# Decoder layer in three stages on one core: GpSimd's second root moves ahead of the addition of the recurrence's input

## The chip, the cores and the metric

The kernel runs on one core of a Trainium2 chip. A core has five engines that work from their own instruction queues: PE (TensorE), DVE (VectorE), ACT (ScalarE), POOL (GpSimd) and SP (SyncE, which only issues DMAs). The metric is the device time of one execution in microseconds (us), the median of several runs.

## The reference

32 sequences of 256 tokens with 256 channels go through three post-norm sublayers:

```
x = layernorm(x + conv.real * x)          # a complex linear recurrence, one state per channel
x = layernorm(x + xattn(x, ctx))          # 16 heads of 16 channels, 256 queries x 256 keys, with its own layer norm
x = layernorm(x + ffn(x))                 # RMS norm, nearest of 8 centroids picks one expert, gated MLP of width 512
```

The recurrence runs over the first axis of `x`, the 32 sequences: `state = c * state + x[n]`, and each needs the one before it. In the third sublayer every token is computed by one expert only, so the kernel sorts tokens by expert.

## The kernel before

Phase 1 (0 to about 850 us of the span) handles one item, a sequence, per step of a software pipeline, for the recurrence, the attention and the choice of the expert. Phase 2 runs the experts on 71 tiles of 128 sorted tokens. There is no scheduler: each engine's program is written out by hand as a function `step(t)`, each operation is for an item t+3, t+2, ... or t-3, and the engines meet through semaphores only (`wait(engine, name, item, per)` before an operation, `then_inc` behind it). So an engine works strictly in the order that its own `step` has, and a wait holds everything that is written behind it.

A step has 16 heads. On PE, head h is `scores` (L1078, into bank S of PSUM, two banks for alternate heads) and `transposed_scores` (L1091, bank T, for the item before). DVE takes the maximum over each S bank (`maxima`, L1312), ACT the exponential of each T bank. Heads are issued in pairs, (0,1), (2,3), and so on, and all the other work of the step stands between the pairs. A bank S is written again only when its maximum has been taken.

The work around the change, in the order of one step:

- DVE, end of step t: the slot of each token of item b = t-3 (L1498, `slot`), the residual y2 of item a = t-2 (L1393), its statistics (L1296) and, behind the maxima of heads 12 to 15, their moments (L1302, written to `mv2`, semaphore `ln2`).
- DVE, start of step t+1: maxima of heads 0 and 1; then `row`, the normalised y2 (L1327, two instructions), which waits for `rstd2`; a copy of the token numbers (L1329); maxima of heads 2 and 3; then `u = (state + 1) * x` (L1335), which waits for all five parts of the recurrence (`conv`).
- POOL, whole step t: `conv_products` (L705, `by_re`, twice as large as the others), `weigh` (L763, `xw`), the bias (L806), `cut` (L794) for the queries, `offset` (L785), `conv_real` (L713), the root for the first layer norm (L738, L740), `conv_imag` (L721, L724) around a `cut` for the keys, the root for the attention's own layer norm (`rstdx`), `scatter` (L775, two indirect DMAs, waits for `slot_ok`), `conv_input` (L731, adds x to `state`), the root for the second layer norm (`rstd2`, L738 and L740) and `rms` (L749 to L755, four tiny operations). The next step begins with L705 again.
- `offset` (L785) writes the constant part of the distances to the centroids. DVE's `pick` (L1461) waits for it behind the maxima of heads 6 and 7. Later in the step DVE adds the queries (L1443) and forms `onehot_bf` (L1478).

`rstd` adds epsilon (L738) and raises to the power of -0.5 (L740):

```
wait(pool, ready, item, per)
g.tensor_scalar(rs[:, 0], mv[:, :, 1], LN_EPS, None, ALU.add).then_inc(s[done], 1)
```

Of the kernel before, what the change touches and what calls it, by code (L numbers as in the profile page):

```python
# [81 lines left out]
def build(nc, x, ctx_in, lmlg, theta, last_conv, Wq, bq, Wk, bk, Wv, bv, ln_g, ln_b, ffn_scale, centroids, up_w, down_w, out):  # L82
    stack = ExitStack()
    with stack:
# [36 lines left out]
        def sb1(name, shape, dt=F32):  # L121
            return phase1.enter_context(nc.sbuf_tensor(name, shape, dt))
# [67 lines left out]
        mv2 = sb1("mv2", [P, NTC, 2])  # L190
        rs2 = sb1("rs2", [P, 2, NTC])
# [38 lines left out]
        def wait(eng, name, item, per=1, j=None):  # L230

            if not item.runtime and item.k >= SEQ:
                item, j = Item(0, SEQ - 1), per
            wait_value(eng, name, item.times(per, per if j is None else j))
# [11 lines left out]
        def wait_ring(eng, sm, item, ring, per):  # L246

            if not item.runtime:
                while item.k >= SEQ:
                    item = item - ring  # L250
            wait_value(eng, sm, item.uses(ring) * per)
# [11 lines left out]
        def active(item):  # L263
            return item.within(0, SEQ)
# [275 lines left out]
        with nc.Block() as block:  # L540
# [121 lines left out]
            def _(pool):  # L662
# [35 lines left out]
                def conv_products(item):  # L698

                    if not active(item):  # L700
                        return
                    wait(pool, "conv", item - 1, 5)
                    if item.k == 1:
                        wait(pool, "x1_ok", item - 1, 2)
                    g.tensor_tensor(by_re[:, :, :, :], state[:, 0].unsqueeze(1).to_broadcast(both), pair_b, ALU.mult).then_inc(s["conv"], 1)  # L705

                def conv_real(item):

                    if not active(item):
                        return  # L710
                    wait(pool, "conv", item, 5, 1)
                    wait(pool, "u_ok", item - 1)
                    g.tensor_tensor(state[:, 0], by_re[:, 1], state[:, 1], ALU.subtract).then_inc(s["conv"], 1)  # L713

                def conv_imag(item, j):

                    if not active(item):
                        return
                    if j == 0:
                        wait(pool, "conv", item, 5, 2)  # L720
                        g.tensor_tensor(state[:, 1], state[:, 1], re_b, ALU.mult).then_inc(s["conv"], 1)  # L721
                    else:
                        wait(pool, "conv", item, 5, 3)
                        g.tensor_tensor(state[:, 1], state[:, 1], by_re[:, 0], ALU.add).then_inc(s["conv"], 1)  # L724

                def conv_input(item):
                    if not active(item):
                        return
                    wait_ring(pool, x_in[item.mod(2)], item, 2, 16)
                    wait(pool, "conv", item, 5, 4)  # L730
                    g.tensor_tensor(state[:, 0], state[:, 0], xt[:, item.mod(2)], ALU.add).then_inc(s["conv"], 1)  # L731

                def rstd(item, ready, per, mv, rs, done):

                    if not active(item):
                        return
                    wait(pool, ready, item, per)
                    g.tensor_scalar(rs[:, 0], mv[:, :, 1], LN_EPS, None, ALU.add).then_inc(s[done], 1)  # L738
                    wait(pool, done, item, 2, 1)
                    g.tensor_tensor(rs[:, 1], rs[:, 0], neg_half[:, :].to_broadcast([P, NTC]), ALU.pow).then_inc(s[done], 1)  # L740

                def rms(item):

                    if not active(item):
                        return
                    p = item.mod(2)
                    wait(pool, "rstd2", item, 2)
                    wait_ring(pool, scat[p], item - 2, 2, 16 * NTC)
                    g.tensor_tensor(ms2[:, 0], mv2[:, :, 1], rs2[:, 1], ALU.mult).then_inc(s["rms"], 1)  # L749
                    wait(pool, "rms", item, 4, 1)  # L750
                    g.tensor_tensor(ms2[:, 1], ms2[:, 0], rs2[:, 1], ALU.mult).then_inc(s["rms"], 1)
                    wait(pool, "rms", item, 4, 2)
                    g.tensor_scalar(ms2[:, 2], ms2[:, 1], RMS_EPS, None, ALU.add).then_inc(s["rms"], 1)
                    wait(pool, "rms", item, 4, 3)
                    g.tensor_tensor(row[:, p, :, C], ms2[:, 2], neg_half[:, :].to_broadcast([P, NTC]), ALU.pow).then_inc(s["rms"], 1)  # L755

                def weigh(item):

                    if not active(item):
                        return  # L760
                    wait(pool, "x2_ok", item, 2)
                    wait(pool, "nx_ok", item - 1, 2)
                    g.tensor_tensor(xw[:, :, :], row[:, item.mod(2), :, 0:C], scale_bc[:, :].unsqueeze(1).to_broadcast([P, NTC, C]),  # L763
                                    ALU.mult).then_inc(s["xw_ok"], 1)

                def scatter(item):

                    if not active(item):
                        return
                    p = item.mod(2)  # L770
                    wait(pool, "slot_ok", item, SLOT)
                    wait(pool, "id_ok", item)
                    wait(pool, "rms", item, 4)
                    for c in range(NTC):
                        g.indirect_dma_start(out=buckets[:, :], out_offset=bass.IndirectOffsetOnAxis(ap=slot[:, p, c:c + 1], axis=0),  # L775
                                             in_=row[:, p, c, :], in_offset=None, bounds_check=PAD - 1,
                                             oob_is_err=False).then_inc(scat[p], 16)

                def offset(item):

                    if not active(item):
                        return
                    wait(pool, "nx_ok", item, 2)
                    wait(pool, "pick", item - 1, PICK, 2)
                    g.tensor_tensor(dist[:, 0], cent_norm[:, :].unsqueeze(1).to_broadcast([P, NTC, E]),  # L785
                                    nx[:, :].unsqueeze(2).to_broadcast([P, NTC, E]), ALU.add).then_inc(s["offset"], 1)

                def cut(item, src, hi, lo, ready, done, out):

                    if not active(item):  # L790
                        return
                    wait(pool, ready, item, 4)
                    wait_ring(pool, out[(item - 1).mod(2)], item - 1, 2, 32)
                    g.tensor_tensor(lo[:, :, :], src, hi[:, :, :].bitcast(F32), ALU.subtract).then_inc(s[done], 1)  # L794

                def step(t):
                    n, a, b = t + 1, t - 2, t - 3
                    first = t.k < 0
                    if first:
                        rstd(t + 2, "ln1", 4, mv1, rs1, "rstd1")  # L800
                    conv_products(t + 3)
                    weigh(b)
                    if active(a):
                        wait(pool, "x1_ok", a, 2)
                        wait(pool, "x1T_pe", a)
                        g.tensor_tensor(x1[:, a.mod(4)], x1[:, a.mod(4)], b_bc[:, :].unsqueeze(1).to_broadcast([P, NTC, C]),  # L806
                                        ALU.add).then_inc(s["x1b_ok"], 1)
                    if n.k > 0:
                        cut(n, q32[:, :, :], q_hi, q_lo, "q_ok", "q_cut", q_out)
                    offset(b)  # L810
                    conv_real(t + 3)
                    if not first:
                        rstd(t + 2, "ln1", 4, mv1, rs1, "rstd1")
                    conv_imag(t + 3, 0)
                    if n.k + 1 > 0:
                        cut(n + 1, k32[:, :, :], k_hi, k_lo, "k_ok", "k_cut", k_out)
                    conv_imag(t + 3, 1)
                    rstd(a, "lnx", 4, mvx, rsx, "rstdx")
                    if t.k < SEQ:
                        scatter(b)  # L820
                    conv_input(t + 3)
                    rstd(a, "ln2", 4, mv2, rs2, "rstd2")
                    rms(a)
                    if t.k >= SEQ:
                        scatter(b)

                steps(pool, step)
                gpsimd2(pool)

# [703 lines left out]
```

## Time and profile before

| | |
|---|---|
| median of 3 runs | 1241.71 us (1241.17 to 1245.56) |
| the profiled execution, own time | 1245.21 us |
| its span in the profile | 1243.4 us |
| mean granted TensorE clock | 0.943 of full speed |
| PE busy | 1110.6 us (89%) |
| DVE busy | 955.3 us (77%) |
| POOL busy | 775.6 us (62%) |
| ACT busy | 668.9 us (54%) |

Busy time is an average over both phases. Phase 1 and phase 2 have different limits, and the change touches phase 1 alone. Times inside the trace are counted from the start of the span.

### The profile page before, as it was taken

The numbers are of one execution on the slowest core, as the hardware profiler recorded it, in microseconds if no ns is written. First come the engines' busy times: TensorE is split into PE (matmuls) and PEld (weight loads), VectorE is DVE, ScalarE is ACT, GpSimd is POOL, SyncE is SP. The second block draws the span as 40 slices with busy tenths as digits, with TensorE's granted clock in tenths as the row PEclk, the third lists the DMA queues.
The fourth block names the chain that finished last, engine by engine and source line by source line (L and its number), as shares of the span: only waits on it lengthen the run. The fifth ranks groups of instructions, "written<-read, shape, count | busy, mean of one in ns | idle before, by whom it ended". The sixth has DMA issues, their size and how long they took to land.

```text
span 1243.4 us, 27486 instructions
## 1 busy us (share of the span) xinstructions
PE 1110.6 (89%) x8030; PEld 818.2 (66%) x8061; DVE 955.3 (77%) x2416; ACT 668.9 (54%) x1416; POOL 775.6 (62%) x932
## 2 busy tenths in 40 slices
PE   3899989999999999989999998853999999999996
PEld 2566666666666666656666666532888888888885
DVE  7458988999989999999999998845555555555553
ACT  4257666767767767767767767541222222222221
POOL 4646879889979888978978955450333333333333
PEclk9679999999999999999999998656999999999998
DMA  4667667766556556556556554042111111111110
GB/s 128 162 162 205 178 179 208 188 148 161 148 134 163 142 142 163 147 138 163 144 141 163 134 130 109 11 153 60 48 51 48 43 51 51 50 47 49 50 52 19
DMA packets 90825, 144.91 MB, mean 117 GB/s; under 512 B 12662, under 2 KB 78335, under 8 KB 84512
## 3 DMA queue, kind: packets, MB, share of 16 engines
q1 hardware_dynamic: 83616, 126.09, 39.2%
q0 software_dynamic: 6528, 16.99, 4.7%
q8 instruction: 55, 0.90, 0.3%
q10 hardware_dynamic: 576, 0.53, 0.2%
q14 instruction: 50, 0.41, 0.1%
HBM read 91.44 MB, written 53.03 MB: 116 GB/s over the span
## 4 chain that ended last, share of the span: by engine, by line
PE 42%; DVE 33%; issue 9%; DMA 6%; POOL 6%; SPq 2%; ACT 1%; POOLq 0%; DVEq 0%; ACTq 0%
DVE neg_max_sb L1312 12%; PE Y L454 10%; PE G L422 8%; PE A L422 8%; DVE oq L1443 4%; DVE u L1335 3%; PE S L1078 3%; DMA neg_max<-nm_row 3%; PE GT L432 2%; PE O L1027 2%; POOL buckets L775 2%; PE M L1035 2%; POOL state L731 2%; DVE st L1296 2%; DVE stx L1296 2%
## 5 line engine op out<-in xcount | busy, mean ns | idle before, releaser
L1312 DVE TENSOR_REDUCE neg_max_sb<-S 128x2 f32<-128x512 f32 x512 | 327.5, 681 | 46.9 <-PE S L1078 46.1
L909 ACT ACTIVATE probs<-T 128x512 f32<-128x512 f32 x512 | 278.1, 595 | 141.0 <-PE T L1091 127.7
L1078 PE MATMUL S<-k_st,q_st 48*128 48x256 f32 x1024 | 215.0, 319 | 38.0 <-DVE neg_max_sb L1312 34.9
L1078 PEld LDWEIGHTS S<-k_st,q_st 48*128 48x128 f32 x1024 | 146.3, 192 | 115.4 <-issue 77.1
L1091 PE MATMUL T<-q_st,k_st 49*128 49x256 f32 x1024 | 211.3, 319 | 6.3 <-DMA q_st<-neg_max 2.6
L1091 PEld LDWEIGHTS T<-q_st,k_st 49*128 49x128 f32 x1024 | 146.4, 192 | 22.8 <-ACT probs L909 15.4
L399 ACT ACTIVATE gT<-GT 128x512 f32<-128x512 f32 x71 | 42.5, 598 | 207.8 <-PE GT L432 207.8
L1027 PE MATMUL O<-probs,v_aug 128*32 128x256 f32 x2048 | 145.6, 404 | 0.8 <-ACT probs L909 0.7
L378 POOL DMA_INDIRECT out<-res,token x71 | 76.5, 1077 | 103.3 <-DVE res L503 98.8
L454 PE MATMUL Y<-dn_sb,gT 128*128 x568 | 134.2, 379 | 0.8 <-ACT gT L399 0.8
L454 PEld LDWEIGHTS Y<-dn_sb,gT 128*128 128x128 f32 x568 | 107.5, 189 | 18.2 <-issue 1.0
L775 POOL DMA_INDIRECT buckets<-row,slot x64 | 67.3, 1052 | 81.9 <-DVE slot L1498 71.8
L422 PE MATMUL G<-up_hi,xsT 128*128 x284 | 107.9, 421 | 1.3 <-DVE xsT L508 1.0
L422 PE MATMUL A<-up_hi,xsT 128*128 x284 | 106.6, 416 | 0.0
L383 POOL TENSOR_SCALAR rs<-mv 128x1 f32<-128x1 f32 x71 | 16.0, 226 | 141.5 <-DVE mv L532 141.4
L503 DVE TENSOR_SCALAR res<-y,mv,rs 128x256 f32<-128x256 f32 x71 | 29.4, 413 | 86.1 <-POOL rs L385 86.1
L1027 PEld LDWEIGHTS O<-probs,v_aug 128*32 128x32 f32 x2048 | 55.4, 113 | 52.8 <-ACT probs L909 16.4
L1035 PE MATMUL M<-ctT,wk_sb 128*128 128x256 f32 x256 | 68.9, 416 | 15.6 <-issue 8.5
L403 ACT ACTIVATE gate<-G 128x512 f32<-128x512 f32 x71 | 42.4, 597 | 59.9 <-PE G L422 59.9
L1054 PE MATMUL M<-wv_sb,ctT 128*128 128x256 f32 x256 | 72.0, 407 | 2.6 <-issue 0.7
L705 POOL TENSOR_TENSOR by_re<-state,decay 128x1024 f32<-128x1024 f32 x31 | 73.5, 2372 | 1.1 <-DVE x L1399 0.9
L1035 PEld LDWEIGHTS M<-ctT,wk_sb 128*128 128x128 f32 x256 | 49.6, 204 | 27.6 <-issue 12.7
(185 smaller groups left out, 2553.9 us busy)
## 6 DMA issues: line engine op xcount, KB each, us to landing
k_st<-k_pieces SPq DMA_DIRECT2D x64, 256.0 KB, 5.1
q_st<-q_pieces SPq DMA_DIRECT2D x64, 256.0 KB, 3.9
xr<-buckets SPq DMA_DIRECT2D x71, 129.0 KB, 2.1
xt<-in_x SPq DMA_DIRECT2D x32, 256.0 KB, 6.1
ct<-in_ctx SPq DMA_DIRECT2D x32, 256.0 KB, 6.8
k_pieces<-k_hi SPq DMA_DIRECT2D x32, 256.0 KB, 3.6
k_pieces<-k_lo SPq DMA_DIRECT2D x32, 256.0 KB, 3.7
q_pieces<-q_hi SPq DMA_DIRECT2D x32, 256.0 KB, 2.1
```

The costliest lines, as they stand in the source:

```text
L378: g.indirect_dma_start(out=out_rows, out_offset=bass.IndirectOffsetOnAxis(ap=token[:, f.mod(2):f.mod(2) + 1], axis=0), in_=res[:, f.mod(2) ...
L422: last = t_.matmul(ps[:, :], xT[:, w, c * P:(c + 1) * P], src[:, bass.ds(off + c * 2 * HID, HID)], start=(k == 0), stop=(k == len(terms) - 1))
L454: last = t_.matmul(Y_ps[:, 0:C], gT[:, m.mod(2), c * P:(c + 1) * P], dn_sb[:, bass.ds(off + c * C, C)], start=(c == 0), stop=(c == HCH - 1))
L705: g.tensor_tensor(by_re[:, :, :, :], state[:, 0].unsqueeze(1).to_broadcast(both), pair_b, ALU.mult).then_inc(s["conv"], 1)
L775: g.indirect_dma_start(out=buckets[:, :], out_offset=bass.IndirectOffsetOnAxis(ap=slot[:, p, c:c + 1], axis=0), in_=row[:, p, c, :], in_of ...
L909: a_.activation(probs[:, h % 8].rearrange("p k t -> p (k t)"), T_ps[h % 2][:, :], ACT.Exp, scale=DH ** -0.5).then_inc(s["exp_ok"], 1)
L1027: last = t_.matmul(O_ps[32 * j:32 * j + 32, (grp % 2) * TOK:(grp % 2 + 1) * TOK], v_aug[:, item.mod(4), kc, h * VW:h * VW + 32], probs[:, ...
L1035: last = t_.matmul(dst[:, oc * TOK:(oc + 1) * TOK], w[:, ic, oc * P:(oc + 1) * P], xT[:, ic, :], start=(ic == 0), stop=(ic == NCH - 1))
L1054: last = t_.matmul(M_ps[1][:, c * C:(c + 1) * C], ctT[:, ic, c * P:(c + 1) * P], wv_sb[:, ic, :], start=False, stop=(c == NTC - 1 and ic = ...
L1078: last = t_.matmul(S_ps[h % 2][:, c * TOK:(c + 1) * TOK], q_st[base:base + STACK, h, c * P:(c + 1) * P], k_st[base:base + STACK, h, :], st ...
L1091: last = t_.matmul(T_ps[h % 2][:, c * TOK:(c + 1) * TOK], k_st[base:base + AUG, h, c * P:(c + 1) * P], q_st[base:base + AUG, h, :], start= ...
L1312: v.tensor_reduce(neg_max[:, cur.mod(2), :, h], S_ps[h % 2][:, :].rearrange("p (c t) -> p c t", c=NTC), AX.X, ALU.max, negate=True).then_i ...
```

## The change

The diff exchanges two calls in GpSimd's step. The root for the second layer norm comes right behind the scatter, and the addition of x to the state comes behind that root. No operation is added, removed or resized, and no wait is.

```diff
                     rstd(a, "lnx", 4, mvx, rsx, "rstdx")
                     if t.k < SEQ:
                         scatter(b)
+                    rstd(a, "ln2", 4, mv2, rs2, "rstd2")
                     conv_input(t + 3)
-                    rstd(a, "ln2", 4, mv2, rs2, "rstd2")
                     rms(a)
```

On POOL, the end of a step in the middle of phase 1 and the start of the next, in the kernel before (`L738`, `L740` with `rs<-mv` are the root, `L731` is the addition of x to the state, `L775` the scatter, `L705` the products of the next item):

```order
L740 TENSOR_TENSOR rsx<-rsx,neg_half 128x2
L775 DMA buckets<-row,slot 66688x258 x2
L731 TENSOR_TENSOR state<-state,xt 128x512
L738 TENSOR_SCALAR rs<-mv 128x2
L740 TENSOR_TENSOR rs<-rs,neg_half 128x2
L749 TENSOR_TENSOR ms<-mv,rs 128x2
L751 TENSOR_TENSOR ms<-ms,rs 128x2
L753 TENSOR_SCALAR ms<-ms 128x2
L755 TENSOR_TENSOR row<-ms,neg_half 128x2
L705 TENSOR_TENSOR by_re<-state,decay 128x1024
```

The same place on POOL in the changed kernel:

```order
L740 TENSOR_TENSOR rsx<-rsx,neg_half 128x2
L775 DMA buckets<-row,slot 66688x258 x2
L738 TENSOR_SCALAR rs<-mv 128x2
L740 TENSOR_TENSOR rs<-rs,neg_half 128x2
L731 TENSOR_TENSOR state<-state,xt 128x512
L749 TENSOR_TENSOR ms<-mv,rs 128x2
L751 TENSOR_TENSOR ms<-ms,rs 128x2
L753 TENSOR_SCALAR ms<-ms 128x2
L755 TENSOR_TENSOR row<-ms,neg_half 128x2
L705 TENSOR_TENSOR by_re<-state,decay 128x1024
```

The two tiny operations of the root have moved ahead of the 128x512 addition. With them the wait for `ln2`, which DVE's moments give, has moved ahead of it too. The programs of PE, DVE and ACT are the same, row for row. DVE's order around it, in both kernels:

```order
L1302 BN_AGGR mv<-st 128x2 x2
L1312 TENSOR_REDUCE neg_max_sb<-S 128x2 x2
L1327 TENSOR_SCALAR row<-oq,mv,rs 128x256 x2
L1329 COPY row<-ids 128x2
L1312 TENSOR_REDUCE neg_max_sb<-S 128x2 x2
L1335 SCALAR_TENSOR_TENSOR u<-state,xt 128x512
```

Nothing has moved here. L1327 is the user of the root and L1335 the user of the addition.

## Rows read from the trace of the kernel before

**Rows 1.** The page: the chain that ended last, shares of the span.

```profile
PE 42%; DVE 33%; issue 9%; DMA 6%; POOL 6%; SPq 2%; ACT 1%; POOLq 0%; DVEq 0%; ACTq 0%
```

**Rows 2.** Busy time of each engine in the stretch 130 to 730 us.

```profile
130.00:730.00 600.00, 553.00 (x4923) 380.72 (x4947) 566.13 (x1432) 426.97 (x941) 513.01 (x564) 0.99 0.61 157
```

The columns are: stretch, its length, busy time of PE, PEld, DVE, ACT and POOL with the number of instructions, granted clock, DMA share, GB/s.

**Rows 3.** Line L1335 (DVE's u): duration ns minimum/median/maximum; busy time, 130 to 730 us.

```profile
L1335 DVE SCALAR_TENSOR_TENSOR u<-state,xt x32: 681/2519/2583, 14.0 to 728.8; 128x512 f32<-128x512 f32 x32
130.00:730.00 600.00, 60.16 (x26) 0.99 0.61 157
```

**Rows 4.** Line L1327 (DVE's row): for whom it waited, us and times.

```profile
  POOL rs L740: 20.6, 29
```

**Rows 5.** Timeline of POOL, 558 to 568.5 us: start, duration, engine, line, operation.

```profile
559.19 1.09 POOL L775 DMA_INDIRECT buckets<-row,slot  x1 [3.26 <-DVE slot L1498]
...
561.58 1.29 POOL L731 TENSOR_TENSOR state<-state,xt 128x512 f32<-128x512 f32 x1
...
563.14 0.72 POOL L740 TENSOR_TENSOR rs<-rs,neg_half 128x2 f32<-128x2 f32 x1
563.94 0.20 POOL L749 TENSOR_TENSOR ms<-mv,rs 128x2 f32<-128x2 f32 x1
...
565.50 2.37 POOL L705 TENSOR_TENSOR by_re<-state,decay 128x1024 f32<-128x1024 f32 x1
```

In brackets stands the idle time ahead of an instruction, and what ended it.

**Rows 6.** Timeline of DVE, 557.9 to 568.5 us.

```profile
558.22 0.16 DVE L1498 CAST slot<-slot_f 128x2 uint32<-128x2 f32 x1
...
561.76 0.24 DVE L1302 BATCH_NORM_AGGREGATE mv<-st 128x2 f32<-128x6 f32 x2
561.92 1.27 DVE L1312 TENSOR_REDUCE neg_max_sb<-S 128x2 f32<-128x512 f32 x2
563.90 0.73 DVE L1327 TENSOR_SCALAR row<-oq,mv,rs 128x256 f32<-128x256 f32 x2 [0.70 <-POOL rs L740]
...
564.68 1.29 DVE L1312 TENSOR_REDUCE neg_max_sb<-S 128x2 f32<-128x512 f32 x2
565.89 2.53 DVE L1335 SCALAR_TENSOR_TENSOR u<-state,xt 128x512 f32<-128x512 f32 x1
```

**Rows 7.** Timeline of PE, 561 to 565 us.

```profile
561.40 0.35 PE L1078 MATMUL S<-k_st,q_st 48*128 48x256 f32 x1 [1.09 <-DVE neg_max_sb L1312]
...
564.37 0.28 PE L1078 MATMUL S<-k_st,q_st 48*128 48x256 f32 x1
```

**Rows 8.** Timeline, 113.2 to 119 us: the first step in which item a exists.

```profile
114.45 0.24 DVE L1302 BATCH_NORM_AGGREGATE mv<-st 128x2 f32<-128x6 f32 x2
...
114.78 0.22 POOL L738 TENSOR_SCALAR rs<-mv 128x2 f32<-128x2 f32 x1 [5.60 <-DVE mv L1302]
...
115.83 0.74 DVE L1327 TENSOR_SCALAR row<-oq,mv,rs 128x256 f32<-128x256 f32 x2
...
117.37 1.29 DVE L1312 TENSOR_REDUCE neg_max_sb<-S 128x2 f32<-128x512 f32 x2 [0.67 <-PE S L1078]
...
117.43 2.37 POOL L705 TENSOR_TENSOR by_re<-state,decay 128x1024 f32<-128x1024 f32 x1
```

**Rows 9.** Timeline, 30.8 to 36 us: a root of 128x2, and what starts behind it.

```profile
31.44 0.72 POOL L740 TENSOR_TENSOR rs<-rs,neg_half 128x2 f32<-128x2 f32 x1
...
32.13 2.35 POOL L705 TENSOR_TENSOR by_re<-state,decay 128x1024 f32<-128x1024 f32 x1
32.19 3.77 DVE L1399 TENSOR_SCALAR x<-u,mv,rs 128x256 f32<-128x256 f32 x2 [1.16 <-POOL rs L740]
```

**Rows 10.** Timeline, 571.5 to 573 us: POOL's offset and DVE's pick.

```profile
571.91 0.21 POOL L785 TENSOR_TENSOR dist<-cent_norm,nx 128x16 f32<-128x16 f32 x1
...
572.24 0.36 DVE L1461 SCALAR_TENSOR_TENSOR dist<-M,row,dist 128x8 f32<-128x8 f32 x2
```

**Rows 11.** Line L1478 (DVE's onehot_bf): duration ns minimum/median/maximum, and its busy time, 130 to 730 us.

```profile
L1478 DVE TENSOR_TENSOR onehot_bf<-expert_no,choice x32: 161/186/1276, 128.3 to 842.5; 128x16 bf16<-128x16 f32 x32
130.00:730.00 600.00, 14.24 (x25) 0.99 0.61 157
```

## The prediction

> **What bounds the kernel now.** I read the page first. The chain that ended last is 42% PE and 33% DVE [rows 1], but that is over two phases, and the change is in the first only. So I took the stretch 130 to 730 us, 26 steps of the steady state (counted by u, 26 times [rows 3]), 600 / 26 = 23.1 us each. There DVE is busy 566.13 us of 600 (94%), PE 553.00 (92%), POOL 513.01 (86%) [rows 2]. Three engines are nearly full, so what matters is which wait of a step ends last, and I read one step, 558 to 568 us, engine by engine.
>
> On POOL the reader is to see a queue without a gap from the scatter on: 559.19 scatter (the only long wait, 3.26 us, for DVE's slot), 561.58 addition to the state, 563.14 root, 563.94 rms, 565.50 by_re, done at 565.50 + 2.37 = 567.87 [rows 5]. On DVE: slot at 558.22, moments done at 561.76 + 0.24 = 562.00, maxima of heads 0 and 1, then row at 563.90 after 0.70 us of waiting for the root, maxima of heads 2 and 3 at 564.68, u at 565.89, which takes 2.53 us [rows 6].
>
> Two things follow. First, u is not working for 2.53 us. It starts 0.39 us behind by_re and ends 0.55 us behind by_re's end (568.42 against 567.87). The same line takes 0.68 us at the least and 2.52 in the median [rows 3]. So the 0.55 us behind by_re are its own streaming, and what is ahead of them is standing. A clearer case of the same thing is early: L1399, whose two instructions take 0.73 us elsewhere, as row's do [rows 6], took 3.77 us when they started 0.06 us behind by_re [rows 9]. A DVE operation of this kind that starts behind a large POOL operation stands until that one ends. In the stretch, u's mean is 60.16 / 26 = 2.31 us [rows 3]; 22 of the 26 that make this sum are over 2.2 us.
>
> Second, row's wait looks like 20.6 us for the taking (29 times, 0.71 us each [rows 4]), but it isn't where the time is lost. The loop that sets a step is: DVE's slot, POOL's scatter to by_re, the end of u, DVE to the next slot. In it POOL has no gap and row doesn't stand.
>
> **The change, part by part.**
>
> *The root comes earlier for DVE.* It can't start when the scatter is done (561.58, where the addition started), since its input is done at 562.00. In the first such step POOL was waiting there, and L738 started at 114.78 for moments done at 114.45 + 0.24 = 114.69, so 0.09 us later [rows 8]. The root starts at 562.09 and takes to 562.09 + 0.32 + 0.72 = 563.13 (L738 to L740 is 0.32: the addition ends at 562.87, its follower starts 0.05 before that end as others of this queue do, at 562.82, and L740 starts at 563.14). That is 0.73 us earlier than 563.86, about all of row's wait. Its worth is nothing: what is behind row is the maximum of head 2, and its scores end on PE at 564.37 + 0.28 = 564.65, against its start at 564.68 [rows 7, 6]. PE worked without a gap from head 1's scores to them. The step at 114 us shows it: there row had no wait, and the maxima waited 0.67 us for PE in its place; from one pair of maxima to the next were 114.61 to 117.37 = 2.76 us, the same as 561.92 to 564.68 [rows 8, 6]. (114.61 is the moments' start 114.45 plus 0.16, as in rows 6.)
>
> *The addition comes later, and with it by_re.* Before, addition, root and rms take 565.50 - 561.58 = 3.92 us to by_re [rows 5]. Afterwards the same work starts at 562.09 instead of 561.58: 0.51 us of POOL waiting, with nothing to cover it. A little comes back, since rms no longer waits for a result just made: from L740 to its dependent L749 are 0.80 us [rows 5], from L740 to an independent by_re only 32.13 - 31.44 = 0.69 [rows 9]. So by_re moves by 0.51 - 0.11 = 0.40 us, to 565.90.
>
> *Row meets the addition.* After the change, row (earliest 563.15) starts about 0.06 us behind the addition (562.09 + 0.32 + 0.69 = 563.10). This is the pattern of rows 9: same form of instruction, same 0.06. L1399's pair there took 3.77 us, and ended each at 0.14 us behind a POOL operation. So row's first half ends at 563.10 + 1.27 + 0.14 = 564.51, against 563.90 + 0.41 = 564.31 before. Maxima of heads 2 and 3 move by 0.20, to 564.88, and u to 566.09. That costs nothing by itself, because u stands behind by_re (565.90) anyway, but its lead decides what follows: by_re is first by 0.19 us.
>
> The Trainium skill, "SBUF — State Buffer", section "SBUF: two separate sides", says that the port pair which DVE and GpSimd share is a lock, held for a whole instruction by whoever starts first, and that a DVE operation with two SBUF inputs needs it against a GpSimd operation that reads SBUF. The trace agrees (3.77 us for 0.73). By that rule alone the order of by_re and u, not their length, sets the price, and the sum below would be the same as long as by_re is first.
>
> *rms meets row's second half.* Bounds: nothing (before, the two overlap too and row takes 0.73 [rows 6]) to about one tiny operation, 0.20 [rows 5]. I take 0.02, near the lower end.
>
> **The sum.** u ends by_re's start + 2.92 (565.50 to 568.42), so each step gets 0.40 + 0.02 = 0.42 us longer, and everything of DVE and POOL behind it moves together. It applies to 22 steps of the stretch and the last u at 728.8 us, 23 in all: 9.7 us. In four steps of the stretch u was short (0.9 to 1.4 us) since PE was late; three of them I count as nothing (bound 0.4 each). The first step has no scatter to wait for: the addition stood in idle time there and moves behind the root, 1.24 us; by_re starts at 117.43 + 1.24, u ends 2.92 behind that start as before: once 1.2 us. Together 10.9 us. The profiled execution would go from 1245.2 to 1256.1; it lay 3.5 us over the median, and against the median it is 1241.7 + 10.9 = 1252.6.
>
> **The rivals.**
>
> *The wait for the root was real: faster (0.08).* If everything on DVE from row on came earlier by row's wait, 26 steps would be 0.70 us shorter each, 18 us: 1223.5. For it speaks that DVE is the busiest engine [rows 2]. The point from which it decides is the end of u: it must come before 568.42. Against it speak PE's end at 564.65, the 0.67 us of waiting at 117.37, and that u ends with by_re, which gets later.
>
> *u overtakes by_re (0.14).* My lead is 0.19 us. If row isn't held up, u is at 565.89 and by_re at 565.90: a tie. Then u takes 0.68 to 566.57 and by_re runs behind it, to about 566.5 + 2.37 = 568.87. The next POOL operation, xw, had to stand behind u's end, 568.42, and now starts at 568.87: 0.45 later, and offset with it. DVE's pick, only 572.24 - 572.12 = 0.12 behind offset's end [rows 10], comes about as much later: 0.45 x 26 + 1 = 12.7 us, 1254.4. DVE's gain of 1.85 us in u turns into waits for PE's scores and for offset. The same page of the Trainium skill, "Who interferes with whom", has it that issue order, not the shape, decides who stands still; the case above is that rule's other outcome.
>
> *The collisions further on change (0.26).* onehot_bf, whose least is 0.16 us, takes up to 1.28 behind a POOL operation. (14.24 - 25 x 0.17) / 1.11 = 9 of 25 steps are long [rows 11], and which of the two engines' waiting operations goes first, with starts some 0.1 us apart, decides it. Phases after by_re stay the same in my forecast, so I expect the same share. If all steps go short (0.10), 9 x 1.11 = 10 us come back: 1242.6, no change. If two thirds go long (0.16), 8 more: 1261.5.
>
> *The chain has slack after all (0.06).* Then the change does nothing: 1241.7. POOL's queue without a gap speaks against it.
>
> *The forecast: 0.46.*
>
> **How the numbers follow.** Half a percent, 6.2 us, is about what a measurement of this kernel tells from no change. Slower by more: 0.46 + 0.14 + 0.16 = 0.76, less 0.05 for a sum that comes out too small (all three bounds at their lower ends give 0.38 x 22 = 8.4, still over 6.2): 0.71. No change: 0.10 + 0.06 + 0.05 = 0.21. Faster: 0.08. The range reaches from the case of all short steps less a little, 1240, to two thirds long plus the upper bound of a step's price (0.60 x 23 = 13.8 for 9.7), 1265. What is left out is the fast rival and a little at both ends.
>
> **What the changed profile would show.** Right if: row's wait for L740 is gone, and row takes about 1.4 us with the addition beside it; the maxima of heads 2 and 3 wait for PE or for row, and start within 2.76 to 3.0 us of those of heads 0 and 1; POOL idles 0.5 us ahead of L738 for DVE's moments; by_re starts 7.68 us behind the start of slot, where it was 565.50 - 558.22 = 7.28; u still takes over 2.2 us. Wrong if u takes 0.7 us (second rival), if onehot_bf's busy time in the stretch moves far from 14 us (third), or if steps get shorter without either (first).

## The result and the profile after

The changed kernel takes **1256.43 us** in the median of four runs (1253.59 to 1262.63), the kernel before 1241.44 in four (1236.99 to 1245.56). The ratio is **1.0128 [1.0075, 1.0182]**: slower by 15.0 us, and the interval leaves out both no change and half a percent. The profiled execution took 1254.54 us, its span is 1252.7, and the mean granted TensorE clock is 0.947, against 0.943 before. A ratio with its interval, here and below, is not the quotient of the two medians given beside it (1.0121 here). Executions that are over 1.5% longer than the fastest one of the same kernel are left out of a ratio, though not out of the medians: four of ten in the third experiment, two of five in the eighth, and one of the 21 of the kernel before in the last four.

The chain that ended last, on the page of the changed kernel:

```profile
DVE 44%; PE 42%; issue 8%; DMA 2%; SPq 1%; ACT 1%; POOL 1%; DVEq 0%; POOLq 0%; ACTq 0%
```

PE has the same 42% as in [rows 1], and DVE has 44% in place of 33%. That is a trap: the engine that the change slowed is POOL, and POOL's share fell to 1%. The chain is followed back along whoever ended a wait. Before, row waited for the root, and there the chain went over to POOL and back to the scatter. Now row waits for nobody, so the chain stays on DVE, where row and u stand behind POOL operations as *busy* instructions, and a busy instruction is put down to its own engine. The stretches below say it more plainly.

Busy time in 130 to 730 us, first of every engine, then of DVE in u (L1335), row (L1327) and onehot_bf (L1478) alone:

```profile
130.00:730.00 600.00, 545.95 (x4867) 375.52 (x4866) 586.77 (x1404) 422.49 (x926) 500.90 (x551) 0.99 0.61 154
...
130.00:730.00 600.00, 71.32 (x25) 0.99 0.61 154
...
130.00:730.00 600.00, 42.39 (x50) 0.99 0.61 154
...
130.00:730.00 600.00, 14.16 (x25) 0.99 0.61 154
```

Against [rows 2], PE and POOL do less in the same 600 us (the steps are longer: u stands in it 25 times for 26), and DVE is busy 586.77 for 566.13 though it too has fewer. The added busy time is standing: u takes 71.32 / 25 = 2.85 us for 60.16 / 26 = 2.31 [rows 3], and row's pair 42.39 / 25 = 1.70 us for 0.73 [rows 6]. onehot_bf is as before: 14.16 for 14.24 [rows 11].

For whom row waited, in the whole run:

```profile
  POOL rs L740: 3.6, 4
```

Before it was 20.6 us in 29 waits [rows 4]. So 17.0 us of DVE's waiting are gone, and the kernel is 15 us slower.

One step on POOL; [rows 5] have the same step of before:

```profile
564.29 1.09 POOL L775 DMA_INDIRECT buckets<-row,slot  x1 [1.60 <-DVE slot L1498]
565.68 0.97 POOL L775 DMA_INDIRECT buckets<-row,slot  x1 [0.30 <-issue]
567.19 0.22 POOL L738 TENSOR_SCALAR rs<-mv 128x2 f32<-128x2 f32 x1 [0.54 <-DVE mv L1302]
567.50 0.72 POOL L740 TENSOR_TENSOR rs<-rs,neg_half 128x2 f32<-128x2 f32 x1
568.20 1.28 POOL L731 TENSOR_TENSOR state<-state,xt 128x512 f32<-128x512 f32 x1
569.44 0.24 POOL L749 TENSOR_TENSOR ms<-mv,rs 128x2 f32<-128x2 f32 x1
...
571.07 2.38 POOL L705 TENSOR_TENSOR by_re<-state,decay 128x1024 f32<-128x1024 f32 x1
```

And on DVE:

```profile
563.32 0.15 DVE L1498 CAST slot<-slot_f 128x2 uint32<-128x2 f32 x1
...
566.87 0.24 DVE L1302 BATCH_NORM_AGGREGATE mv<-st 128x2 f32<-128x6 f32 x2
567.02 1.27 DVE L1312 TENSOR_REDUCE neg_max_sb<-S 128x2 f32<-128x512 f32 x2
568.25 1.70 DVE L1327 TENSOR_SCALAR row<-oq,mv,rs 128x256 f32<-128x256 f32 x2
...
569.94 1.27 DVE L1312 TENSOR_REDUCE neg_max_sb<-S 128x2 f32<-128x512 f32 x2
571.14 2.85 DVE L1335 SCALAR_TENSOR_TENSOR u<-state,xt 128x512 f32<-128x512 f32 x1
...
577.81 0.36 DVE L1461 SCALAR_TENSOR_TENSOR dist<-M,row,dist 128x8 f32<-128x8 f32 x2
```

The reader is to see four things. POOL idles 0.54 us ahead of L738, where it had no gap. by_re starts 571.07 - 563.32 = 7.75 us behind slot, for 7.28 in [rows 5, 6]. Row starts 0.05 us behind the addition (568.25 against 568.20) and takes 1.70 us without a wait. u starts 0.07 behind by_re and ends at 573.99, 0.54 behind by_re's end (573.45); it was 0.55 before. pick (L1461) follows at 14.49 behind slot, for 14.02 in [rows 6, 10]. The 0.47 us at by_re, which is where the change ends on POOL, is found again 7 us later without loss. From the first u of the steady part to the last, 26 steps later, are 115.1 to 737.5 = 622.4 us, before 118.6 to 728.8 = 610.2: 12.2 us more, 0.47 a step. The two profiled spans differ by only 9.3 us, since the profiled execution of the changed kernel came to that first u 3.5 us earlier.

The steps aren't all of one length, and the shortest ones tell the change best: from one by_re to the next they are 22.69 us before and 23.15 after. Over the 24 steps from 141.45 to 704.32 us before, and from 138.51 to 714.24 after, the changed kernel takes 12.86 us more, of which 24 x 0.46 = 11.0 us is this floor. The other 1.8 us lie in the steps that are longer than it, by a long onehot_bf or by a late PE.

### The profile page after: what moved, and what is told of

Its sections match the earlier page's. It is cut to its first block, busy times and chain, and to the rows that moved or that the text cites. A ratio compares the mean times of both kernels' runs of the same rounds, so it can differ in the third digit from the quotient of the medians.

```text
span 1252.7 us, 27516 instructions
## 1 busy us (share of the span) xinstructions
PE 1110.0 (89%) x8060; PEld 816.2 (65%) x8061; DVE 990.2 (79%) x2416; ACT 671.8 (54%) x1416; POOL 770.9 (62%) x932
## 4 chain that ended last, share of the span: by engine, by line
DVE 44%; PE 42%; issue 8%; DMA 2%; SPq 1%; ACT 1%; POOL 1%; DVEq 0%; POOLq 0%; ACTq 0%
DVE neg_max_sb L1312 17%; PE Y L454 10%; PE G L422 8%; PE A L422 8%; DVE oq L1443 4%; PE M L1035 3%; DVE u L1335 3%; DVE st L1296 3%; DVE row L1327 3%; PE S L1078 3%; PE GT L432 2%; DVE oq L1393 2%; PE O L1027 2%; DVE x L1399 2%; DVE stx L1296 2%
## 5 line engine op out<-in xcount | busy, mean ns | idle before, releaser
L1312 DVE TENSOR_REDUCE neg_max_sb<-S 128x2 f32<-128x512 f32 x512 | 326.5, 679 | 38.7 <-PE S L1078 38.5
L1078 PE MATMUL S<-k_st,q_st 48*128 48x256 f32 x1024 | 212.2, 315 | 41.3 <-DVE neg_max_sb L1312 38.1
L1078 PEld LDWEIGHTS S<-k_st,q_st 48*128 48x128 f32 x1024 | 143.7, 189 | 118.2 <-issue 78.3
L775 POOL DMA_INDIRECT buckets<-row,slot x64 | 67.3, 1051 | 84.9 <-DVE slot L1498 74.9
L1035 PE MATMUL M<-ctT,wk_sb 128*128 128x256 f32 x256 | 76.1, 449 | 29.2 <-issue 22.7
L1035 PEld LDWEIGHTS M<-ctT,wk_sb 128*128 128x128 f32 x256 | 54.4, 223 | 43.3 <-issue 27.7
L1335 DVE SCALAR_TENSOR_TENSOR u<-state,xt 128x512 f32<-128x512 f32 x32 | 79.3, 2477 | 0.0
L705 POOL TENSOR_TENSOR by_re<-state,decay 128x1024 f32<-128x1024 f32 x31 | 73.6, 2376 | 1.2 <-DVE x L1399 0.9
```

What stands on the lines that cost most here:

```text
L1035: last = t_.matmul(dst[:, oc * TOK:(oc + 1) * TOK], w[:, ic, oc * P:(oc + 1) * P], xT[:, ic, :], start=(ic == 0), stop=(ic == NCH - 1))
L1078: last = t_.matmul(S_ps[h % 2][:, c * TOK:(c + 1) * TOK], q_st[base:base + STACK, h, c * P:(c + 1) * P], k_st[base:base + STACK, h, :], st ...
L1312: v.tensor_reduce(neg_max[:, cur.mod(2), :, h], S_ps[h % 2][:, :].rearrange("p (c t) -> p c t", c=NTC), AX.X, ALU.max, negate=True).then_i ...
L1335: v.scalar_tensor_tensor(u[:, :, :], state[:, 0], 1.0, xt[:, nn.mod(2)], ALU.add, ALU.mult).then_inc(s["u_ok"], 1)
```

## The experiments

In the experiments "before" is the kernel before, run again on the same chip. All numbers relative to slot are from steps near 560 us. In the changed kernel every step of the stretch repeats them within 0.03 us: by_re starts 7.74 to 7.76 us behind slot, pick 14.47 to 14.52.

### The wait alone, without the move

The order of before; only the wait for DVE's moments is put ahead of the addition. Line numbers behind it are 2 higher.

```diff
                         scatter(b)
+                    if active(a):
+                        wait(pool, "ln2", a, 4)
                     conv_input(t + 3)
                     rstd(a, "ln2", 4, mv2, rs2, "rstd2")
```

What was expected:

> The order of the kernel before, with one thing of the change alone: GpSimd waits for the moments (ln2) ahead of the addition to the state; the root stays behind the addition, so vector's row isn't served earlier and doesn't meet the addition. Theory one (the wait in GpSimd's gapless queue from the scatter to by_re is the cost): by_re comes about 0.5 us later behind slot (7.28 becomes 7.8), u still takes over 2.5 us, row waits some 1.2 us for the root in place of 0.70, a short step is 22.68 + 0.5 = 23.2 us, and the run is about 12 us slower than before, as the changed kernel. Rival (row's collision with the addition, 1.70 us for 0.73, is the cost): here row takes 0.73, and the time is that of the kernel before within 3 us.

Measured: 1261.26 us (1258.22 to 1265.13, 4 runs), before 1245.92 (13 runs), ratio **1.0132 [1.0101, 1.0163]**. POOL's timeline of this kernel:

```profile
570.35 1.27 POOL L731 TENSOR_TENSOR state<-state,xt 128x512 f32<-128x512 f32 x1 [0.53 <-DVE mv L1304]
571.60 0.22 POOL L738 TENSOR_SCALAR rs<-mv 128x2 f32<-128x2 f32 x1
...
574.26 2.38 POOL L705 TENSOR_TENSOR by_re<-state,decay 128x1024 f32<-128x1024 f32 x1
```

DVE's timeline of the same step:

```profile
566.48 0.16 DVE L1500 CAST slot<-slot_f 128x2 uint32<-128x2 f32 x1
...
572.65 0.74 DVE L1329 TENSOR_SCALAR row<-oq,mv,rs 128x256 f32<-128x256 f32 x2 [1.19 <-POOL rs L740]
...
574.57 2.62 DVE L1337 SCALAR_TENSOR_TENSOR u<-state,xt 128x512 f32<-128x512 f32 x1
```

by_re starts 7.78 us behind slot. Nothing was reordered, row isn't held by the addition (0.74), and the slowdown is that of the changed kernel. So the 0.53 us for which POOL waits for the moments is a sufficient cause. Row's collision with the addition isn't needed for it.

### The root and rms both ahead of the addition

```diff
                         scatter(b)
-                    conv_input(t + 3)
                     rstd(a, "ln2", 4, mv2, rs2, "rstd2")
                     rms(a)
+                    conv_input(t + 3)
```

What was expected:

> Root, then rms, then the addition to the state, all behind the scatter. The same total of GpSimd's work behind the same wait, but only tiny operations beside row. Theory one: by_re as in the changed kernel (7.7 behind slot); row takes 0.73 and the maxima of heads 2 and 3 wait for PE; u needs the addition, which ends about when by_re can start, so the two meet; time 8 to 15 us over the kernel before. Rival (row's collision is the cost): about the kernel before. Second rival (row's gain of 0.7 us is worth something as long as nothing eats it): up to 18 us faster than before, since row's wait is gone here with no collision in its place.

Measured: 1260.46 us (1257.58 to 1263.91, 4 runs), ratio **1.0108 [1.0080, 1.0135]**. DVE's timeline:

```profile
568.50 0.16 DVE L1498 CAST slot<-slot_f 128x2 uint32<-128x2 f32 x1
...
573.45 0.74 DVE L1327 TENSOR_SCALAR row<-oq,mv,rs 128x256 f32<-128x256 f32 x2
...
574.98 1.29 DVE L1312 TENSOR_REDUCE neg_max_sb<-S 128x2 f32<-128x512 f32 x2 [0.66 <-PE S L1078]
576.42 2.91 DVE L1335 SCALAR_TENSOR_TENSOR u<-state,xt 128x512 f32<-128x512 f32 x1 [0.15 <-issue]
```

Here row has neither a wait nor a collision. It is done 0.66 us before the maxima of heads 2 and 3 can start, and they wait for PE's scores in its place. So an early row is worth nothing, as the prediction had it, and the kernel is as slow as with the collision. What both share is POOL's wait; by_re starts 7.90 behind slot.

### The addition ahead of the scatter

```diff
+                    conv_input(t + 3)
                     if t.k < SEQ:
                         scatter(b)
-                    conv_input(t + 3)
                     rstd(a, "ln2", 4, mv2, rs2, "rstd2")
```

What was expected:

> The addition to the state stands ahead of the scatter, in the 1.6 to 3.3 us in which GpSimd waits for slot; behind the scatter only root and rms. Theory one: by_re comes about 6.5 us behind slot in place of 7.28, so u ends some 0.7 us earlier, less about 0.5 us that the addition takes from vector's two-input operations beside it (L1450, L1393): 0 to 10 us faster than before, most likely 5. Row's wait is gone and the maxima of heads 2 and 3 wait 0.6 us for PE. Rival (row's wait was the price, whatever by_re does): 18 us faster than before. If GpSimd's queue isn't what sets the step: slower than before by the new collisions, some 10 us.

Measured: 1254.47 us in the median of ten runs (1238.54 to 1268.99), which scatter more than those of any other kernel here; ratio **1.0015 [0.9977, 1.0054]**. The median of all ten lies 0.7% above the kernel before, and the longest had a granted clock of 0.919 where the shortest had 0.938. Whether the kernel brings that about itself isn't shown, so a small loss isn't excluded. POOL's timeline:

```profile
535.70 1.27 POOL L731 TENSOR_TENSOR state<-state,xt 128x512 f32<-128x512 f32 x1
537.81 1.09 POOL L775 DMA_INDIRECT buckets<-row,slot  x1 [0.84 <-DVE slot L1498]
...
540.72 0.22 POOL L738 TENSOR_SCALAR rs<-mv 128x2 f32<-128x2 f32 x1 [0.55 <-DVE mv L1302]
...
543.38 2.37 POOL L705 TENSOR_TENSOR by_re<-state,decay 128x1024 f32<-128x1024 f32 x1
```

DVE's slot in the same step:

```profile
536.35 0.65 DVE L1498 CAST slot<-slot_f 128x2 uint32<-128x2 f32 x1
```

POOL still waits 0.55 us for the moments, but the addition's 1.24 us are out of the chain and lie where POOL waited for slot. In return slot itself stands 0.49 us behind the addition (0.65 us for 0.16). The sum is 7.75 - 1.24 + 0.49 = 7.00 from slot to by_re; 543.38 - 536.35 = 7.03 was measured. The expectation had 6.5: it had the addition hold up other operations of DVE, not slot itself. It was 7.28 in the kernel before, but only about 0.1 us of the 0.25 comes through to the shortest steps (22.5 to 22.6 us for 22.7), and no gain is measured: PE is next. The maxima wait for it 36.8 us in the stretch (35 times). Before it was:

```profile
  PE S L1078: 8.4, 9
```

### u ahead of row, in the kernel before

DVE's u moves from behind the maxima of heads 2 and 3 to ahead of row, so that it runs before by_re starts.

```diff
                             maxima(cur, h + 1)
+                        if h == 0 and active(nn):
...
+                            v.scalar_tensor_tensor(u[:, :, :], state[:, 0], 1.0, xt[:, nn.mod(2)], ALU.add, ALU.mult).then_inc(s["u_ok"], 1)
                         if h == 0 and active(b):
                             wait(dve, "rstd2", b, 2)
...
-                        if h == 3 and active(nn):
...
-                            v.scalar_tensor_tensor(u[:, :, :], state[:, 0], 1.0, xt[:, nn.mod(2)], ALU.add, ALU.mult).then_inc(s["u_ok"], 1)
```

What was expected:

> GpSimd as before; vector computes u ahead of row, in the 0.70 us in which it waited for the root, and so ahead of by_re. If by_re and u standing in one another's way is what makes u 2.5 us long: u takes 0.7 to 1.4 us here and row is at most 0.7 us later, the maxima of heads 4 and 5 start up to 0.65 us earlier (then PE's scores stop them), xw isn't behind u any more and offset comes 0.4 us earlier; pick waits for offset. A step gets 0.4 to 0.5 us shorter, the run about 11 us faster than before, 1230 us. If u's length is its own and not by_re's: u takes 2.5 us here too and the run is slower than before by up to 2 us a step.

Measured: 1256.44 us (1254.46 to 1259.28, 4 runs), ratio **1.0091 [1.0067, 1.0114]**. The expectation of a gain was wrong. DVE's timeline:

```profile
569.48 0.68 DVE L1328 SCALAR_TENSOR_TENSOR u<-state,xt 128x512 f32<-128x512 f32 x1
570.78 0.74 DVE L1333 TENSOR_SCALAR row<-oq,mv,rs 128x256 f32<-128x256 f32 x2 [0.62 <-POOL rs L740]
...
574.08 1.29 DVE L1312 TENSOR_REDUCE neg_max_sb<-S 128x2 f32<-128x512 f32 x2 [1.28 <-PE S L1078]
...
578.66 0.36 DVE L1461 SCALAR_TENSOR_TENSOR dist<-M,row,dist 128x8 f32<-128x8 f32 x2 [0.52 <-POOL dist L785]
```

POOL's timeline of the same step:

```profile
569.50 1.24 POOL L740 TENSOR_TENSOR rs<-rs,neg_half 128x2 f32<-128x2 f32 x1
...
572.38 2.37 POOL L705 TENSOR_TENSOR by_re<-state,decay 128x1024 f32<-128x1024 f32 x1
```

Line L1478 (onehot_bf) in 130 to 730 us, with the minimum, median and maximum duration in ns:

```profile
L1478 DVE TENSOR_TENSOR onehot_bf<-expert_no,choice x25: 163/1248/1267, 149.3 to 727.4; 128x16 bf16<-128x16 f32 x25
```

u takes 0.68 us for 2.5, so DVE is 1.8 us earlier there. All of it goes: u starts 0.02 us ahead of the root, and the root takes 1.24 us for 0.72, so by_re comes 7.80 behind slot (slot is at 564.58), 0.5 later than before. The maxima of heads 4 and 5 then wait 1.28 us for PE, pick waits 0.52 us for POOL's offset, and onehot_bf is long nearly always: 29.12 us in the stretch where it was 14.24, and its median is 1248 ns for 186 [rows 11]. Not all of these cost the same. At pick only 0.06 us of the half microsecond at by_re is left (578.66 - 564.58 = 14.08 behind slot for 14.02), since xw no longer stands behind u, while onehot_bf is long in 23 of 25 steps for 9, 14 more at 1.1 us. That is the bulk of the slowdown. So both mechanisms that the second and the third rival name exist, one engine or the other going first and a different share of long onehot_bf; the change under study starts neither.

### The changed kernel with earlier moments, and its control

If POOL's wait is the cause, the change must cost nothing once the moments are there in time. On DVE the statistics of y2 are taken ahead of x1 (L1399) and the moments ahead of the maxima of heads 14 and 15, in the changed kernel and, as a control, in the kernel before.

```diff
+                        if h == 13 and active(a):
+                            wait(dve, "y_ok", a, 4)
+                            stats(a, y2, st2, "ln2")
                         if h == 13 and active(nn):
                             wait(dve, "rstd1", nn, 2)
...
                         if h == 13 and active(a):
-                            wait(dve, "y_ok", a, 4)
-                            stats(a, y2, st2, "ln2")
-                        if h == 14 and active(a):
                             moments(a, st2, mv2, "ln2")
```

What was expected of the changed kernel with it:

> The changed kernel's order on GpSimd, but vector takes the statistics of y2 right behind y2 and their moments ahead of the maxima of heads 14 and 15, about 1.1 us earlier, so that GpSimd has nothing to wait for when it comes from the scatter. Row still meets the addition. Theory one (GpSimd's wait for ln2 is the cost): the wait of 0.54 us ahead of L738 is gone, by_re comes 7.2 to 7.3 us behind slot as in the kernel before, pick at about 14.0, and the run is within 4 us of the kernel before. Rival (row's collision with the addition is the cost): row still takes about 1.7 us and the run stays 12 us over the kernel before.

What was expected of the kernel before with it:

> The control of the last one: the same edit on vector, GpSimd's order as before. Both theories: by_re 7.28 behind slot, row's wait 0.7 as before (the root follows the addition, not the moments), the maxima of heads 14 and 15 some 0.15 us later, time within 3 us of the kernel before. Theory one has the last kernel and this one within 3 us of each other, the rival has them 12 us apart.

Measured, both in 11 runs, with before at 1242.25 (21 runs): 1241.48 us, ratio **1.0011 [0.9985, 1.0037]**, for the changed kernel; 1242.25 us, ratio **1.0024 [0.9990, 1.0058]**, for the control. The two medians lie 0.77 us apart, within the 3 us of theory one, where the rival had 12. POOL and then DVE of the changed kernel with early moments, in one step:

```profile
553.39 0.97 POOL L775 DMA_INDIRECT buckets<-row,slot  x1 [0.30 <-issue]
554.39 0.24 POOL L738 TENSOR_SCALAR rs<-mv 128x2 f32<-128x2 f32 x1
...
555.42 1.27 POOL L731 TENSOR_TENSOR state<-state,xt 128x512 f32<-128x512 f32 x1
...
558.27 2.37 POOL L705 TENSOR_TENSOR by_re<-state,decay 128x1024 f32<-128x1024 f32 x1
```

```profile
551.03 0.16 DVE L1498 CAST slot<-slot_f 128x2 uint32<-128x2 f32 x1
...
556.09 1.07 DVE L1327 TENSOR_SCALAR row<-oq,mv,rs 128x256 f32<-128x256 f32 x2
557.65 1.29 DVE L1312 TENSOR_REDUCE neg_max_sb<-S 128x2 f32<-128x512 f32 x2 [0.42 <-PE S L1078]
558.86 2.33 DVE L1335 SCALAR_TENSOR_TENSOR u<-state,xt 128x512 f32<-128x512 f32 x1
```

L738 follows the scatter without a wait, and by_re is 558.27 - 551.03 = 7.24 behind slot, 0.51 less than in the changed kernel. The loss is gone, with the changed order still in place. And nothing is gained: the maxima behind row wait 0.42 us for PE.

One thing did not come as expected: row still meets the addition and has no wait, but it starts 0.67 us behind it, not 0.05, and takes 1.07 us, where about 1.7 was expected. So this kernel lacks most of row's standing as well as POOL's wait, and it can't tell the two apart by itself. The first two experiments do: there row takes 0.74 us, POOL's wait is in place, and the loss is there in full.

In the control by_re comes as in the kernel before, 567.25 - 559.97 = 7.28 behind slot:

```profile
559.97 0.16 DVE L1498 CAST slot<-slot_f 128x2 uint32<-128x2 f32 x1
...
567.25 2.36 POOL L705 TENSOR_TENSOR by_re<-state,decay 128x1024 f32<-128x1024 f32 x1
```

### The addition ahead of the scatter, and u ahead of the maxima of heads 0 and 1

A try at a faster kernel: the third experiment's POOL order, with u moved ahead of the maxima of heads 0 and 1, so that it meets the scatter and not the root or by_re.

```diff
+                    conv_input(t + 3)
                     if t.k < SEQ:
                         scatter(b)
-                    conv_input(t + 3)
...
+                        if h == 0 and active(nn):
...
+                            v.scalar_tensor_tensor(u[:, :, :], state[:, 0], 1.0, xt[:, nn.mod(2)], ALU.add, ALU.mult).then_inc(s["u_ok"], 1)
                         if h % 2 == 0:
                             maxima(cur, h)
...
-                        if h == 3 and active(nn):
...
-                            v.scalar_tensor_tensor(u[:, :, :], state[:, 0], 1.0, xt[:, nn.mod(2)], ALU.add, ALU.mult).then_inc(s["u_ok"], 1)
```

What was expected:

> A try at a faster kernel: the addition ahead of the scatter (as in the third experiment) and u ahead of the maxima of heads 0 and 1, where GpSimd waits for the moments, so that u and by_re don't meet. Theory one: u takes 0.7 us, the maxima of heads 2 and 3 start where PE lets them (6.46 behind slot), those of heads 4 and 5 0.6 us earlier than before, pick at 13.6 in place of 14.0; a short step 22.2 us, the run 10 us faster than before, unless onehot_bf is long in nearly every step, which would cost 1.1 x 16 = 18 us more. Rival (u's collision isn't worth anything, PE sets the step): no difference beyond the third experiment, whose ratio was 1.0015.

And the same with the early moments:

> The last kernel with the early moments as well: by_re some 0.5 us earlier again (6.0 to 6.5 behind slot), offset no longer near pick. Time as the last kernel or up to 4 us less, since pick is then held by PE's scores and not by offset; the collisions of onehot_bf fall anew and can be worth 10 us either way.

Measured: 1259.15 us (1256.36 to 1266.26, 5 runs), ratio **1.0153 [1.0110, 1.0196]**, and with early moments 1280.44 (1265.42 to 1292.62, 5 runs), ratio **1.0208 [1.0151, 1.0266]**. The seventh was expected some 10 us faster than the kernel before, the eighth as fast as the seventh or up to 4 us faster still; both expectations were wrong. What was aimed at on DVE was reached: u takes 0.66 us in the seventh and 0.68 in the eighth, and DVE is busy 524.84 and 505.40 us of 600 for 566.13 (with fewer maxima in it, 403 and 388 for 410). On POOL it was not: in the eighth by_re starts 6.8 or 7.3 us behind slot, where 6.0 to 6.5 was expected. Both kernels are slower, and what they wait for is PE. The stretch 130 to 730 us of the eighth:

```profile
130.00:730.00 600.00, 557.93 (x4693) 377.75 (x4718) 505.40 (x1363) 407.81 (x896) 498.81 (x533) 0.93 0.58 150
```

PE alone in single microseconds of one of its steps (stretch, its length, busy time of PE, granted clock, DMA share, GB/s):

```profile
537.00:538.00 1.00, 0.53 (x5) 1.00 0.44 131
538.00:539.00 1.00, 0.19 (x2) 1.00 0.96 156
...
541.00:542.00 1.00, 1.00 (x13) 0.50 0.72 113
...
544.00:545.00 1.00, 1.00 (x6) 1.00 0.29 92
```

For whom its maxima (L1312) waited in 130 to 730 us:

```profile
  PE S L1078: 87.3, 48
```

PE had 1.28 us without work ahead of 538.8. About 1.2 us later its granted clock fell to 0.50, that is the lower of its two levels (1.2 GHz), for some 3 us, and it was back at 2.4 GHz at 544. Over the stretch the granted clock is 0.93 for 0.99. The clock falls like this in 20 of the eighth's 24 steps of the stretch, in the kernel before 3 times and in the changed one 5 times. The maxima waited 87.3 us for PE where it was 8.4 before. Why the clock falls in these steps and not in others isn't settled: the seventh has an idle time of 1.51 us at the same place both in steps in which it falls and in steps in which it stays at 1.00.

## Why the prediction was right

**The root comes earlier, at no gain.** Right. Row's wait went from 20.6 us to 3.6, and it was worth nothing. The second and the fifth experiment show it with less in the way of row: with row done early, the maxima of heads 2 and 3 wait 0.66 and 0.42 us for PE's scores.

**The addition comes later, and by_re with it.** Right, and this step is the loss. POOL waits 0.54 us, where the prediction had this work 0.51 us late. From slot to L738 are 3.87 us, as predicted (562.09 - 558.22). The 0.11 us that come back hold as well: from L740 to the addition are 0.70 us, from the addition to rms 1.24. The first experiment shows that the wait alone does it, the fifth that without the wait the loss is gone as far as the runs tell (ratio at most 1.0037).

**Row meets the addition.** The mechanism was right. The size was misread in one place: the sum had row's first half at 1.36 us and its end at 0.20 late, which with the second half's 0.32 is 1.68 for the pair; the "about 1.4" of the list is the first half alone. Measured were 1.70 for the pair, the longest half 1383 ns, and the maxima of heads 2 and 3 followed those of heads 0 and 1 by 2.92 us, within the 2.76 to 3.0 forecast. The Trainium skill, "SBUF — State Buffer", section "SBUF: two separate sides", says that the one that starts first keeps the shared ports for a whole instruction and the other stands still. The trace agrees in both directions: row's first half ends 0.15 us behind the addition's end, and in the fourth experiment POOL's 128x2 root, started 0.02 us behind u, takes 1.24 us for 0.72.

**rms meets row's second half.** Too small: 0.02 us predicted, 0.07 measured. From L749 to by_re are 571.07 - 569.44 = 1.63 us, before 1.56. It stayed within its bounds (0 to 0.20). With it by_re comes 7.75 behind slot, where 7.68 was forecast (that number leaves out the 0.02; the sum has 7.70), and its lead over u was 0.07 us instead of 0.19. That lead carried the forecast: u started behind by_re and took 2.85 us, but with 0.07 us more the other way it would have been a tie, the case of the second rival. That so thin a lead held is in part luck, though it held in all 25 steps of the stretch.

**The sum.** 0.47 us a step for 0.42. Over 23 steps that is 10.8 us for 9.7, and 12 with the start's 1.2. That one came true: in the first such step by_re starts 115.00 - 110.83 = 4.17 us behind the moments' start, where it was 117.43 - 114.45 = 2.98 [rows 8]. Between the first u and the last, which doesn't hold the start, were 12.2 us more. The sum counted three steps with a late PE as nothing; in the changed kernel no u of the stretch is short (2.84 to 2.86 us all), so the price is paid in those as well. Against the median, 15.0 us were measured for 10.9, with an interval of 9 to 23 us (1.0075 and 1.0182 times 1241.44), so that what is left of the difference is within the spread of the runs.

**The rivals.** The wait was real: no, 17 us of it went and the kernel got slower. u overtakes by_re: no, its median is 2850 ns. The collisions further on change: no, 14.16 us for 14.24 [rows 11], 9 long ones in 25 before and after. That the two are so equal is in part luck: in the first experiment, which slows the step in the same way, it was 11.69 us, 7 long ones in 24. The chain has slack: no, 0.47 us at by_re is 0.47 us at pick.

## What to carry to other kernels

Look for the queue without a gap, not for the longest wait: a wait that the chain shows on one engine (20.6 us here) may be backed by another engine that is late by nearly as much, while 0.5 us of waiting put into a queue without a gap cost 0.5 us in every step. When an operation is moved ahead, compare the time at which its input is there with the time at which the queue gets to it, and count what then stands behind its wait. If the move is wanted all the same, bring the input forward first; and an operation that two engines' shared ports hold up shows as busy, so read its mean against its least before calling an engine full.

## What the runs showed of the hardware

A 128x2 operation of GpSimd can stand behind one of VectorE as well: the root took 1.24 us for 0.72 when u (128x512, two inputs) had started 0.02 us ahead. In the cases read here, with starts 0.02 to 0.07 us apart, it was the engine ahead that ran and the other that stood, and a small shift elsewhere can turn nearly all steps of a kernel the same way: onehot_bf was long in 9 of 25 steps before, and in 23 of 25, 29.12 us for 14.24, when u was moved to another place in the step. And taking u's standing off VectorE (0.68 us for 2.5, the engine busy 505.40 us of the stretch for 566.13) did not make this kernel faster: it got slower, with TensorE at a granted clock of 0.93 in the stretch for 0.99.
